# A state-space layer and a mixture of experts in one kernel: TensorE's projections on other slots of the chunk loop

## What is computed

```python
xz = x @ in_proj_w.T;  xc, z = split(xz)                # 512 + 512
u  = conv1d(xc, conv_w) + conv_b                        # 4 taps, 512 -> 512, causal
dt = clip(sigmoid(u @ dt_w.T + dt_b), 1e-4, 1)
Bm, Cm = u @ B_w.T, u @ C_w.T                           # 16 + 16
for every token t:                                      # state: 512 x 16
    state = exp(dt*A) * state + dt*B*u + 1e-6
    y = sum(state * C) + D*u
x = x + (y * silu(z)) @ out_w.T
x = x + experts(norm(x)) + sigmoid(gate) * shared_ffn(norm(x))
```

## Time and profile before

| | us |
|---|---|
| median of 3 runs | 2993.37 |
| lowest, highest | 2986.91, 2995.44 |
| the profiled execution, its own time | 2990.34 |
| its span in the trace | 2988.5 |
| chunks: first to last gating of y (31 steps) | 134.0 to 2316.2 |
| tiles, after the chunks | about 670 |

### The profile page before, as it was taken

The page is one execution under the profiler, slowest core; times in us unless marked ns, Lnnn a source line. Parts: engine busy times, 40 slices in busy tenths (PEclk is TensorE's granted clock), DMA queues, the critical chain, the costliest instruction groups (busy, mean ns, idle before and its releaser), DMA issues. The chain is left out here.

```text
span 2988.5 us, 49244 instructions
## 1 busy us (share of the span) xinstructions
PE 2630.8 (88%) x15616; PEld 2312.5 (77%) x15616; DVE 2249.8 (75%) x4890; ACT 2033.5 (68%) x4675; POOL 2235.5 (75%) x1354
## 2 busy tenths in 40 slices
PE   7888898889888888988988888898886599999998
PEld 4777787778777777877877877887875488888887
DVE  2999889988998999899889989998999233333332
ACT  3987888888878888788878878888876133333332
POOL 2999888988888889889889988898887033333333
PEclk9999989998999888899899899888997699999999
DMA  4222222222222222222222222222221278888886
GB/s 168 82 75 76 75 82 76 75 75 90 88 80 79 75 79 89 76 76 85 79 76 75 76 82 75 75 89 87 78 74 41 75 199 201 202 201 202 198 204 152
DMA packets 138185, 309.67 MB, mean 104 GB/s; under 512 B 15041, under 2 KB 79681, under 8 KB 137793
## 3 DMA queue, kind: packets, MB, share of 16 engines
q1 hardware_dynamic: 110848, 270.03, 28.9%
q0 software_dynamic: 27072, 36.46, 6.2%
HBM read 258.42 MB, written 48.01 MB: 103 GB/s over the span
## 5 line engine op out<-in xcount | busy, mean ns | idle before, releaser
L1032 POOL TENSOR_TENSOR room<-dtu,b_all 128x1024 f32<-128x1024 f32 x512 | 1202.3, 2371 | 32.4 <-DVE dtu L1420 14.1
L810 ACT ACTIVATE bank<-room,eps_col 128x512 f32<-128x512 f32 x1024 | 695.2, 685 | 294.6 <-DVE carry L1257 200.3
L794 ACT ACTIVATE room<-room,neg_a 128x256 f32<-128x256 f32 x2048 | 868.8, 499 | 0.8 <-DVE room L1209 0.8
L600 PE MATMUL bank<-ident,room 128*128 128x128 f32 x4096 | 550.9, 291 | 242.7 <-DVE room L1252 220.1
L600 PEld LDWEIGHTS bank<-ident,room 128*128 128x128 f32 x4096 | 495.3, 150 | 295.9 <-DVE room L1252 238.8
L1021 POOL TENSOR_TENSOR room<-room,c_all 128x1024 f32<-128x1024 f32 x224 | 530.9, 2370 | 159.3 <-DVE bank L1243 59.8
L1243 DVE TENSOR_TENSOR_SCAN bank<-room,carry,bank 128x256 f32<-128x256 f32 x864 | 580.3, 735 | 54.5 <-ACT bank L810 53.7
L1157 POOL DMA_INDIRECT out<-room,ids x144 | 223.8, 1554 | 410.1 <-DMA out<-room,ids 192.9
L1322 DVE SCALAR_TENSOR_TENSOR hid<-hid,bank 128x256 f32<-128x256 f32 (+1 forms) x312 | 131.0, 420 | 453.5 <-ACT hid L905 421.2
L1243 DVE TENSOR_TENSOR_SCAN room<-room,carry,bank 128x256 f32<-128x256 f32 x672 | 445.7, 726 | 0.7 <-DVE hot L1293 0.5
L552 PE MATMUL bank<-xnT,w_conv 128*128 128x256 f32 x3072 | 404.2, 288 | 7.0 <-ACT xnT L833 5.5
(11 more groups left out here) (150 smaller groups left out, 3151.0 us busy)
## 6 DMA issues: line engine op xcount, KB each, us to landing
b_all<-b_scratch SPq DMA_DIRECT2D x128, 512.0 KB, 3.9
c_all<-b_scratch SPq DMA_DIRECT2D x128, 512.0 KB, 5.1
room<-in_wgu SPq DMA_DIRECT2D x72, 704.0 KB, 5.8
room<-in_wd SPq DMA_DIRECT2D x72, 384.0 KB
room<-x_by_expert SPq DMA_DIRECT2D x72, 260.0 KB
x_in<-in_x SPq DMA_DIRECT2D x32, 256.0 KB, 5.9
x<-in_x SPq DMA_DIRECT2D x32, 256.0 KB, 2.7
out<-x SPq DMA_DIRECT2D x32, 256.0 KB, 4.2
```

Source lines behind the costliest of these rows:

```text
L600: last = mm(tr_bank[k][:, b * P:(b + 1) * P], v[n % VRING][:, b, k * P:(k + 1) * P], ident[:, :], is_transpose=True, start=False, stop=(n ...
L794: last = af(da[n % RING][:, b, :], dt[c.par][:, b, :], ACT.Exp, scale=neg_a[:, b, n:n + 1])
L810: af(v_slot(c, n, h)[:, :], v[n % VRING][:, 2 * h:2 * h + 2, :].rearrange("p b t -> p (b t)"), ACT.Identity, bias=eps_col[:, 0:1]).then_in ...
L1032: nc.gpsimd.tensor_tensor(out=v[n % VRING][:, :, :], in0=dtu[:, :, :], in1=row, op=ALU.mult) \
```

## The change

For chunk `proj`, the pieces of work move to other slots. The first convolution piece runs in slot 15 of the call before (where the chunk is still `norm`), behind everything else of that slot on PE, the second stays first in slot 0, the third and fourth go from slots 3 and 4 to 4 and 5; B and C from 5 to 7; dt from 6, 7 to 7, 8; z from 9, 10 to 10, 11. ScalarE's uT moves from slots 2, 5 to 1, 6, its other parts one slot later, and so do VectorE's. The shared expert's gate_up and gates go one slot later, to 12 to 14 and 13 to 15. `low_normed` goes one slot earlier, to 14, where it stands ahead of the gate. No instruction is added or taken away.

```diff
-GU_SLOT, GATE_SLOT = [11, 12, 13], [12, 13, 14]
+GU_SLOT, GATE_SLOT = [12, 13, 14], [13, 14, 15]
-CONV_SLOT, Z_SLOT = [0, 1, 3, 4], [9, 10]
+CONV_SLOT, Z_SLOT = [0, 4, 5], [10, 11]
+DT_SLOT, BC_SLOT = [7, 8], 7
...
                 if slot in CONV_SLOT:
-                    n = CONV_SLOT.index(slot)
+                    n = CONV_SLOT.index(slot) + 1
                     proj_conv(c, n // 2, n % 2)
...
+                        if norm and slot == 15:
+                            proj_conv(norm, 0, 0)
...
-                if slot in (2, 5):
-                    h = slot // 3
+                if slot in (1, 6):
+                    h = slot // 6
...
-                if slot in (7, 8):
+                if slot in (8, 9):
...
-                if slot == 6:
+                if slot == 7:
...
-                if slot in (10, 11):
+                if slot in (11, 12):
...
-                        if proj and slot in (8, 9):
-                            proj_dt(proj, slot - 8)
-                        if proj and slot == 11:
+                        if proj and slot in (9, 10):
+                            proj_dt(proj, slot - 9)
+                        if proj and slot == 12:
                             proj_gate(proj, 0)
                             proj_gate(proj, 1)
-                        if norm and slot == 15:
+                        if norm and slot == 14:
                             low_normed(norm)
```

More of the change, by code:

```diff
@@ L692, in project @@
                 if slot in CONV_SLOT:
-                    n = CONV_SLOT.index(slot)
+                    n = CONV_SLOT.index(slot) + 1
                     proj_conv(c, n // 2, n % 2)
-                if slot == 5:
+                if slot == BC_SLOT:
                     proj_bc(c)
-                if slot in (6, 7):
-                    proj_dt(c, slot - 6)
+                if slot in DT_SLOT:
+                    proj_dt(c, DT_SLOT.index(slot))
                 if slot in Z_SLOT:
@@ L724, in start @@
                     pe.wait_ge(w_early, 16 * EARLY_LOADS)
+                    proj_conv(Chunk(0, 0), 0, 0)
                     for slot in range(NS):
@@ L727, in start @@
                     proj_norm(Chunk(0, 1))
+                    proj_conv(Chunk(0, 1), 0, 0)
                 def __call__(self, scan, post, proj, norm):
@@ L845, in project @@
                     last.then_inc(evac, 1)
-                if slot in (7, 8):
-                    h = slot - 7
+                if slot in (8, 9):
+                    h = slot - 8
                     act.wait_ge(pr_ready, done + 5 + h)
@@ L859, in project @@
                     act.sem_inc(b_ready, 1)
-                if slot in (10, 11):
-                    k = slot - 10
+                if slot in (11, 12):
+                    k = slot - 11
                     act.wait_ge(pr_ready, done + 7 + k)
@@ L928, in start @@
                         project(Chunk(0, 0), slot)
-                        if slot == 8:
+                        if slot == 9:
                             decays(Chunk(0, 0), 0)
```

## The result

The changed kernel takes 3044.05 us (median of 4 runs, 3042.36 to 3044.87), the kernel before 2993.19: a ratio of 1.0173, 95% interval 1.0155 to 1.0190. That is 51 us slower, and the chunks are where they go: from the first gating of y to the last it is 52.5 us more.

The account below looks back on a forecast made before the run. No single engine was the bound: four, 82 to 90% busy, lose time in handovers, counted by VectorE's waits. Order changes of +0.4 and the clock's +1.3 gave 1.7 us per chunk, x 30 = +51 us; stated 3040, range 2965 to 3085.

Parts of the forecast that it names:

- (b): Slot 7: VectorE's wait for add_eps shrinks from 1.7 to 1.15 us, since uT comes after both halves: -0.55 per chunk.
- (g): Slot 7: TensorE idles 3.1 us ahead of B and C, its clock falls in seven of ten chunks: +1.3 us per chunk.
- (a): Slots 1 to 4: one convolution piece fewer ahead of post_y and post_out; VectorE's post_out wait goes: -0.9 us per chunk.
- (c): Slot 8: VectorE's wait for tanh of dt goes, since it asks one slot later: -0.6 us per chunk.
- (d): Slot 12: ScalarE falls behind, waiting for TensorE's dt path, and VectorE's wait for zs grows: +1.1 us per chunk.
- (e): Slots 13 to 15: low_normed waits 1.3 us and the gate of slot 15 waits 0.45: +1.35 us per chunk.
- (f): Slot 15: the moved convolution piece costs no one anything and wins little; at half clock it takes 6.1 us.
- 2 (clock stays up): Rival: the clock stays up in the 3.1 us gap; only +0.4 us per chunk, 3000 to 3012 us; chance 0.22.
- 3 (a fall at each chunk, y held up): Rival: clock falls longer, every chunk; last transposes delay VectorE's gating of y; +3.2 us per chunk, 3086 us; chance 0.17.
- 4 (zs not waited for): Rival: faster; ScalarE reaches zs before VectorE; with the clock up -1.1 us per chunk, 2957 us; chance 0.18.

Follow-up runs that it names:

- a_fill: The changed kernel with 20 extra matmuls per chunk on TensorE directly ahead of B and C, their result overwritten: 3015.34 us.
- b_later: The kernel before with only convolution pieces, uT, B and C, dt and z in later slots; first piece, low_normed and gates as before: 3001.03 us.
- a_low_zs: The changed kernel with low_normed behind the gate of slot 14 and the second proj_gate in slot 13, without extra matmuls: 2975.14 us.
- b_piece: The kernel before with the first convolution piece in slot 15 of the call before, low_normed in 14 ahead of the gate, uT's first half in 1: 3027.42 us.

## Why the prediction was right, point by point

**The sum.** 3040 was stated, 3044 measured; +1.7 us per chunk was forecast and +1.70 measured. Two of its terms, (b) and (g), were off by some 0.4 us each in opposite directions, so that the agreement to 4 us is in part luck.

**(a) post_out, (c) tanh of dt.** Right in place and size: 0.82 to 0, 0.69 to 0.05.

**(b) add_eps in slot 7.** Wrong in its effect. -0.55 was forecast, +0.09 measured for all add_eps waits, and -0.17 in a_fill, where the clock does not fall at B and C. The waits of slot 7 did go, further than I had it: VectorE waits 0.18 us there in the chunk shown above, where it waited 1.73 in that of the earlier trace rows. But other halves wait instead (99 waits of 0.67 us in the stretch, for 78 of 0.85); in this chunk slot 9 has 1.05 us of them for 0.70:

```profile
1180.19 1.39 DVE L1248 TENSOR_TENSOR_SCAN bank<-room,carry,bank 128x256 f32<-128x256 f32 x2 [0.18 <-ACT bank L815]
...
1185.67 1.39 DVE L1248 TENSOR_TENSOR_SCAN bank<-room,carry,bank 128x256 f32<-128x256 f32 x2 [0.34 <-ACT bank L815]
1187.78 1.39 DVE L1248 TENSOR_TENSOR_SCAN bank<-room,carry,bank 128x256 f32<-128x256 f32 x2 [0.71 <-ACT bank L815]
```

The step priced one slot and took those behind it to stay as they were.

**(d) zs.** Right in size: +1.1 forecast, +1.18 measured. That the wait is on VectorE's path is shown by moving proj_gate alone, 47 us; that it comes with the later slots, by b_later (+0.98). The reason given, ScalarE held by TensorE's dt path, is not shown: in a_fill ScalarE waits 1.1 us per chunk less for dt, and the wait for zs does not shrink.

**(e) low_normed and the gates.** Right: 1.30 measured for low_normed against 1.3, 0.95 for the two gates against 0.95. The edit that puts low_normed behind the gate takes off 24 us.

**(f) the moved piece.** Right that it costs no one: VectorE waited for y's transposes 0.2 us in the whole stretch. The piece waits 4.1 us per chunk for its bank, so the idle slot is not filled but moved, and in most chunks it runs below full clock (4.38 us in the mean for 3.10; 6.1 was the forecast's worst case).

**(g) the clock.** The idle time was 2.89 us (3.1 forecast), the clock fell in 22 of 30 chunks (seven in ten), and taking the fall away gained 29 us (39 forecast). The step that failed is the last one, "all of it reaches zs": a_fill left the wait for zs as it was. B and C take 1.4 us more in such a chunk, dt's two halves mostly ran at full clock again, and the loss showed at the routing product and at add_eps, waits of VectorE ahead of zs that (g) does not have. (The 29 us are net of whatever the slower piece in slot 15 costs.) The Trainium skill ("TensorE: Matmul & The Clock Gate", Part 1: The HAM clock gate) has the ramp penalty, for modelling, at under 1% of a typical kernel's span. What the matmuls in the gap ahead of B and C gain is 29 of 3044 us in the changed kernel, just under that, and 51 of 2975 us, 1.7%, in the order of a_low_zs: there the measurement differs, and it decides.

**The rivals.** 2 (clock stays up) falls by the windows and the count. 3 (a fall at each chunk, y held up) by the count and by VectorE's waits. 4 (zs not waited for) by the waits; its test, dt's second half ready when ScalarE comes, fails: ScalarE waited 74.1 us for dt in the stretch, 3.0 per chunk.

**What the prediction did not see** is that the shared gates' move is a gain alone. Its two halves, read from the waits, are not open to the full change: the moved convolution piece has already taken post_out's wait, and low_normed no longer stands ahead of the third gate. No run takes the gates' move out of the changed kernel.

## What to carry to other kernels

- In a loop in which several engines are 80 to 90% busy, price a move of work by the wait that it makes on the engine that runs ahead, not by the idle slot that it fills: zs (1.2 us per chunk more), low_normed (0.8) and an idle gap that slows the clock (0.9) outweighed the two waits that went, and undoing them with three small edits (one of them 20 matmuls per chunk that compute nothing) gave a kernel faster than both.
- Work whose result is not needed at once belongs behind the instruction that the longest path waits for, and where something else covers its own wait: moving 0.8 us of VectorE's gate behind the last state's product and behind low_normed gained 41 us, about half of it at post_out and nearly as much from the gate's own wait.
- Savings that name the same wait can be had once. And where a queue is idle for some 3 us in each round, look at TensorE's clock behind it before calling the idle time free.

## What the runs showed of the hardware that I had not expected

- Matmuls of no use placed in a 2.9 us gap shortened this kernel by 1.0% and 1.7%: the clock stayed at 2.4 GHz in the matmuls right behind them. In a_fill the clock of the whole stretch hardly rose for that (0.93 after 0.92), as it fell in another place. Placed in a gap that is 0.5 us too short for them they cost 18 us (30 against 20 of them).
- The same gap does not always slow the clock: after 2.88 or 2.89 us of idling it fell in 21 of 22 chunks of the changed kernel (not in that of 528 us), and in 19 of 26 of a_low_zs. After the 2.30 to 2.46 us of six other chunks of the changed kernel it did not fall. But in b_piece gaps of 2.33 us were followed by a fall, and in b_later so were 15 of 21 gaps of 2.05 to 2.09 us, behind different mixes of work. What makes the difference was not tested.
